# A four-layer attention kernel on one core: x and weight transfers, the q and k projections and the normalisation's small steps placed at other tiles

## The chip, the core and the metric

The kernel runs on one core of a Trainium2 chip. The metric is the device time of one execution in microseconds (us), lower is better; the time before is the median of three runs.

## The reference, cut to what matters

Four layers of multi-head attention with a decomposed relative position bias, each on the group-normalised input and added back to it. Two images of 48x48 tokens, 192 channels, 12 heads of 16 channels.

```python
for layer in range(4):
    h = group_norm(x, groups=32)                 # over a group's 6 channels and all 2304 tokens
    q, k, v = split(h @ Wqkv + bqkv)             # 12 heads of 16
    attn = (q * 16 ** -0.5) @ k.T                # 2304 x 2304 per head and image
    attn += rel_h[:, :, None] + rel_w[:, None]   # q @ Rh, q @ Rw
    x = x + concat(softmax(attn) @ v) @ Wproj + bproj
```

## The kernel before, in words

**Work.** A layer and an image are a stage (8 stages, `s`), a head of a stage is a unit (96 units, `u = 12 s + j`, with `j` the head). A unit is 18 tiles (`t`), each of 128 keys against all 2304 queries. Of each tile TensorE makes five score matmuls (L750; 512, 512, 512, 512, 256 columns), ScalarE takes their exponentials (L535), and one tile later TensorE multiplies them with v (`attend`, L829). In the same tile five more matmuls (L759) form scores of the next unit but one or the next, of which VectorE takes the maxima (L639) that the exponent is shifted by. Scores and maxima alternate through two rings of three PSUM banks, one drained by ScalarE and one by VectorE.

**The written order.** `schedule()` (L53) gives each unit, tile and slot (0 to 5) its items, and TensorE, ScalarE and VectorE all walk the same table. Beside the maxima there are: in tiles 0 to 11 a `rel` item (L775, the bias tables of unit u + 2, copied by ScalarE at L518 and L523); in tile 14 the `mt` item (L781, the maxima turned into a row, written to `mrow` by ScalarE at L545); and `late` items in slot 0 of tiles 12 to 17. These are, by head: 1 and 2, `fin` (output projection of the stage before, L813, added to x by VectorE at L646); 3, `gn` (the normalisation's group sums, L786); 4 to 6, `qk` (projections to q and k of the next stage, L794, copied by ScalarE at L557); 7 and 8, `v` (L802).

**Normalisation.** For the next stage, at head 3, VectorE takes twelve `stat` (L598), one in each of tiles 0 to 11, then `aggregate`, `group_mean`, and at tile 15 `group_scale` (L615), 19 steps on 96x2 elements, each of which waits for the one before (`link`). `normalise` (L630, 96x2304, two of them) runs at head 4, tiles 1 and 2, slot 3, when x has been stored.

**q and k.** ScalarE writes a projection to `stage`, GpSimd splits it into a high and a low part (`split`, L489 and L491), SyncE sends both to `qk_scratch` (`qk_store`, L372). There are two buffers: ScalarE waits for the split two before, the split for the store two before. On GpSimd a unit's six splits come after `normalise(u - 1)` (L481) and the six `low` (L476).

**The transfer queue.** All transfers are issued by SyncE in one written order (L392 to L454). At each tile it waits until the tile's scores are made, then sends a row of bias for three tiles on (`row_load`, L306; needed by the scores of that tile). At tile 3 it loads the first third of the next unit's q and bias (`slot_load`, L312, L314, L306), at tile 15 the second, at 16 the third, and with them the row of maxima (`top_load`, L323, from `mrow`): thirds 0 and 1 at tile 15, 2 at tile 16. Before a unit's tile 0, at head 0, come the load of x (L246, one transfer of 1728 KB) and, every second stage, four transfers of weights (L256); at head 3 the store of x (L252); the last stage's x is loaded ahead of head 8. At tile 12 `image_load`, at 13 and 14 `rel_store`. `qk_store` of heads 4 to 6 stands at tiles 14 to 17 and at tiles 0 and 1 of the next unit.

The excerpt that waits first at a unit's start, from `ready_for_scores` (L730):

```python
if i == 0:
    slot, use = slot_of(u, third)
    pe.wait_ge(slot_in[slot], 144 * use + 64 + 16 * c)   # q, bias, row and mrow of this third
```

Of the kernel before, what the change touches and what calls it, by code (L numbers as in the profile page):

```python
# [40 lines left out]
MSPLIT = SPLIT[-1:] + SPLIT[:-1]  # L41
MT_AT = 2
SLOTS = 4
VCOL = DH + 1
# [8 lines left out]
def schedule():  # L53


    plan = {u: [[[] for _ in range(6)] for _ in range(TILES)] for u in range(-3, UNITS + 2)}

    first = [("gn", 0, 0), ("gn", 0, 1)] + [("qk", 0, m, g) for m in range(3) for g in range(NB)] \
        + [("v", 0, k) for k in range(QT // 2)]
    for k, item in enumerate(first):  # L60
        plan[-3][k // 2][k % 2].append(item)
    for u in range(-2, UNITS):
        for t in range(TILES):
            n, q = (u + 1, t + KEEP) if t < TILES - KEEP else (u + 2, t + KEEP - TILES)
            if 0 <= n < UNITS:
                for m in range(MAXB):
                    plan[u][t][m].append(("max", n, q, m))
            if t < 12 and u + 2 < UNITS:
                plan[u][t][0].append(("rel", u + 2, t))
        if 0 <= u + 1 < UNITS:  # L70
            plan[u][TILES - KEEP][MT_AT].insert(0, ("mt", u + 1))
        s, j = divmod(u, HEADS)
        if u < 0:
            continue
        late = []
        if s >= 1 and j in (1, 2):
            late = [("fin", s - 1, 3 * (j - 1) + g, m) for g in range(3) for m in range(2)]
        elif s + 1 < STAGES and j == 3:
            late = [("gn", s + 1, 0), None, None, ("gn", s + 1, 1)]
        elif s + 1 < STAGES and 4 <= j < 7:  # L80
            late = [("qk", s + 1, j - 4, g) for g in range(NB)]
        elif s + 1 < STAGES and 7 <= j < 9:
            late = [("v", s + 1, k) for k in range(6 * (j - 7), min(6 * (j - 6), QT // 2))]
        for k, item in enumerate(late):
            if item:
                plan[u][12 + k][0].append(item)
    last = [("fin", STAGES - 1, g, m) for g in range(NB) for m in range(2)]
    for k, item in enumerate(last):
        plan[UNITS + 1][k][0].append(item)
    return plan  # L90
# [21 lines left out]
def build(nc, a):  # L112
# [3 lines left out]
    with ExitStack() as ctx:  # L116
# [122 lines left out]
        def _(sp):  # L239
            def x_of(s):  # L240
                l, b = divmod(s, IMAGES)
                src = a["x"] if l == 0 else x_dram
                return src[:, b * N:(b + 1) * N].rearrange("(t p) n -> p t n", t=2)

            def x_load(s):
                sp.dma_start(xb[:, :, :], x_of(s)).then_inc(x_in, 16)  # L246

            def x_store(s):

                sp.wait_ge(dve_read, place["fin", s, NB - 1, 1] + 1)  # L250
                dst = (x_dram if s + IMAGES < STAGES else a["out"])[:, (s % IMAGES) * N:(s % IMAGES + 1) * N]
                sp.dma_start(dst.rearrange("(t p) n -> p t n", t=2), xb[:, :, :]).then_inc(x_stored, 16)  # L252

# [123 lines left out]
            x_load(0)  # L377
            weights(0)
# [13 lines left out]
            for u in range(-2, UNITS):  # L392
                s, j = divmod(u, HEADS) if u >= 0 else (-1, -1)
                if j == 0:
                    sp.wait_ge(for_dve, place["v", s, QT // 2 - 1] + 1)
                    x_load(s - 1 if s else 1)
                    if s % 2 and s + 1 < STAGES:
                        sp.wait_ge(dve_read, place["v", s, QT // 2 - 1] + 1)
                        weights((s + 1) // 2)
                if j == 5 and s % 2 == 0 and s:  # L400
                    sp.wait_ge(for_dve, place["fin", s - 1, NB - 1, 1] + 1)
                    sp.wait_ge(dve_read, place["fin", s - 1, NB - 1, 1] + 1)
                    proj_weights(s // 2)
                if j == 3 and s:
                    x_store(s - 1)
                if u == UNITS - 4:
                    sp.wait_ge(x_stored, 16 * (STAGES - 1))
                    x_load(STAGES - 1)
                for t in range(TILES):
# [15 lines left out]
                    if t == 8 and u >= 0 and u + 2 < UNITS:  # L425
                        mkeys_load(u + 2)
                    if t == 5 and u >= 1:
                        rec_store(u - 1)
# [30 lines left out]
            for g in range(NB):  # L459
                ao_load(STAGES - 1, g)  # L460
            x_store(STAGES - 1)
            sp.wait_ge(x_stored, 16 * STAGES)


        @block.gpsimd
        def _(pool):
# [30 lines left out]
            for u in range(-2, UNITS):  # L497
                s, j = divmod(u, HEADS) if u >= 0 else (-1, -1)
                if u >= 1:
# [72 lines left out]
        def _(dve):  # L572
# [19 lines left out]
            def stat(s, k):  # L592
# [3 lines left out]
                else:  # L596
                    dve.wait_ge(x_in, 16 * (s + 1))
                return dve.bn_stats(stats[:, m, g, :], xb[:, m, g * BLK:(g + 1) * BLK])  # L598
# [15 lines left out]

            def group_scale(bank):  # L615

                link(dve.tensor_scalar(gv[:, :], bank[0:HALF, 0:2], EPS, None, ALU.add))
                link(dve.tensor_scalar(gr[:, :].bitcast(I32), gv[:, :].bitcast(I32), -0.5, SEED, ALU.mult, ALU.add))
                for _ in range(4):
                    link(dve.tensor_tensor(gt[:, :], gr[:, :], gr[:, :], ALU.mult))  # L620
                    link(dve.tensor_tensor(gt[:, :], gt[:, :], gv[:, :], ALU.mult))
                    link(dve.tensor_scalar(gt[:, :], gt[:, :], -0.5, 1.5, ALU.mult, ALU.add))
                    link(dve.tensor_tensor(gr[:, :], gr[:, :], gt[:, :], ALU.mult))
                link(dve.scalar_tensor_tensor(out=gn[:, :], in0=gm[:, :], scalar=-1.0, in1=gr[:, :],
                                              op0=ALU.mult, op1=ALU.mult))

            def normalise(s, m):
                if s >= 2:
                    dve.wait_ge(x_stored, 16 * (s - 1))
                dve.tensor_scalar(xb[:, m, :], xb[:, m, :], gr[:, m:m + 1], gn[:, m:m + 1], ALU.mult, ALU.add)\  # L630
                    .then_inc(xn_ready, 1)

            def consume(item):
# [7 lines left out]
                elif item[0] == "fin":  # L641
                    _, s, g, m = item
                    if g == 0 and m == 0:
                        dve.wait_ge(x_in, 16 * (s + 3 if s + 1 < STAGES else STAGES + 2))
                    xs = xb[:, m, g * BLK:(g + 1) * BLK]
                    dve.scalar_tensor_tensor(out=xs, in0=bank[0:HALF, 0:BLK], scalar=bproj[:, m:m + 1], in1=xs,  # L646
                                             op0=ALU.add, op1=ALU.add).then_inc(dve_read, 1)
                elif item[0] == "gn":
# [3 lines left out]
                    else:  # L652
                        group_scale(bank)
                        dve.sem_inc(dve_read, 1)  # L654
# [37 lines left out]
            for u in range(-3, UNITS + 2):  # L692
                s, j = divmod(u, HEADS) if 0 <= u < UNITS else (-1, -1)
                for t in range(TILES):
                    for i in range(SB + 1):
                        if s + 1 < STAGES and j == 3:
                            if i == 1 and t < 12:
                                last = stat(s + 1, t)
                            if i == 0 and t == 12:
                                aggregate(s + 1, last)  # L700
                        for item in plan[u][t][i]:
                            if item[0] not in ON_ACT:
                                consume(item)
                            if item == ("gn", 0, 1):
                                normalise(0, 0)
                                normalise(0, 1)
# [198 lines left out]
```

## Time and profile before

| what | before |
|---|---|
| median of 3 runs | 7275.24 us (7269.46 to 7281.24) |
| the profiled execution's own time | 7286.74 us |
| its span | 7285.0 us |
| mean granted TensorE clock | 0.978 |
| PE, DVE, ACT, POOL busy | 95%, 75%, 64%, 13% |
| mean DMA rate | 139 GB/s, queue 1 busy 60.8% |

The span runs from the first to the last instruction of one execution; the 1.7 us around it belong to its own time. A busy share is the union of an engine's instructions over the span. TensorE is called PE, VectorE DVE, ScalarE ACT, GpSimd POOL and SyncE's queue SPq. The granted clock is a share of 2.4 GHz.

### The profile page before, as it was taken

The numbers are of one execution on the slowest core, as the hardware profiler recorded it, in microseconds if no ns is written. First come the engines' busy times: TensorE is split into PE (matmuls) and PEld (weight loads), VectorE is DVE, ScalarE is ACT, GpSimd is POOL, SyncE is SP. The second block draws the span as 40 slices with busy tenths as digits, with TensorE's granted clock in tenths as the row PEclk, the third lists the DMA queues.
The fourth block names the chain that finished last, engine by engine and source line by source line (L and its number), as shares of the span: only waits on it lengthen the run. The fifth ranks groups of instructions, "written<-read, shape, count | busy, mean of one in ns | idle before, by whom it ended". The sixth has DMA issues, their size and how long they took to land.

```text
span 7285.0 us, 139171 instructions
## 1 busy us (share of the span) xinstructions
PE 6943.9 (95%) x53600; PEld 4318.7 (59%) x53600; DVE 5490.2 (75%) x10165; ACT 4652.3 (64%) x10033; POOL 931.5 (13%) x967
## 2 busy tenths in 40 slices
PE   6999999999999999999999999999999999999998
PEld 4655656556565565656656566565665656656654
DVE  5776777767777677877878778787777877777773
ACT  2666666666666666666666666666666666666665
POOL 2111111120101101011101111111101021111110
PEclk8999999999999999999999999999999999999999
DMA  5566566556665666656666656666566665566664
GB/s 142 128 138 146 134 139 145 140 141 139 137 152 131 151 130 146 144 133 145 131 147 143 147 137 140 139 152 142 130 141 137 149 145 138 132 146 143 137 135 95
DMA packets 306018, 1013.72 MB, mean 139 GB/s; under 512 B 107152, under 2 KB 196688, under 8 KB 215632
## 3 DMA queue, kind: packets, MB, share of 16 engines
q1 hardware_dynamic: 305360, 1004.81, 60.8%
q8 instruction: 429, 7.03, 0.5%
q14 instruction: 229, 1.88, 0.1%
HBM read 745.26 MB, written 255.69 MB: 137 GB/s over the span
## 4 chain that ended last, share of the span: by engine, by line
PE 88%; DMA 4%; DVE 3%; issue 2%; SPq 2%; POOL 1%; ACT 1%; POOLq 0%; ACTq 0%; DVEq 0%
PE work L759 29%; PE work L750 25%; PE work L829 25%; PE work L775 4%; DMA qk_scratch<-back 2%; DMA moving<-rel_scratch 2%; PE work L813 2%; PE work L794 1%; DVE mpart L639 1%; PE work L802 1%; SPq L372 1%; PE work L781 0%; POOL back L491 0%; ACT back L557 0%; DVE xb L630 0%
## 5 line engine op out<-in xcount | busy, mean ns | idle before, releaser
L639 DVE TENSOR_REDUCE mpart<-work 128x1 f32<-128x512 f32 (+1 forms) x8640 | 5087.1, 632 | 1490.7 <-PE work L759 1472.8
L535 ACT ACTIVATE probs<-work 128x512 f32<-128x512 f32 (+1 forms) x8640 | 4045.6, 558 | 927.5 <-PE work L750 910.4
L750 PE MATMUL work<-moving,keys 113*128 113x512 f32 (+1 forms) x8640 | 3433.3, 398 | 233.7 <-issue 96.1
L759 PE MATMUL work<-mkeys,hi 128*128 128x512 f32 (+1 forms) x8640 | 3472.9, 403 | 32.0 <-DVEq L654 19.3
L759 PEld LDWEIGHTS work<-mkeys,hi 128*128 128x128 f32 x8640 | 1660.5, 192 | 1183.8 <-DVE mpart L639 834.9
L750 PEld LDWEIGHTS work<-moving,keys 113*128 113x128 f32 x8640 | 1657.9, 192 | 778.4 <-ACT probs L535 199.1
L829 PE MATMUL work<-probs,vall 128*17 128x288 f32 x27648 | 2047.7, 415 | 0.0
L829 PEld LDWEIGHTS work<-probs,vall 128*17 128x17 f32 x27648 | 642.0, 97 | 801.7 <-ACT probs L535 226.9
L476 POOL TENSOR_TENSOR full<-full,hi 128x384 f32<-128x384 f32 x576 | 579.7, 1007 | 1662.1 <-DVE hi L682 1662.1
L518 ACT ACTIVATE full<-work 48x384 f32<-48x384 f32 x576 | 279.1, 485 | 642.3 <-PE work L775 642.3
L481 POOL TENSOR_TENSOR rden<-oraw,rden 128x576 f32<-128x576 f32 x96 | 136.2, 1418 | 4167.0 <-DMA rden<-inverse_scratch 4167.0
L523 ACT ACTIVATE full<-work 48x384 f32<-48x384 f32 x576 | 278.9, 484 | 585.2 <-PE work L775 585.2
L775 PE MATMUL work<-image,tab 128*48 128x48 f32 (+1 forms) x6912 | 497.5, 215 | 4.9 <-DMA image<-qk_scratch 4.9
L775 PEld LDWEIGHTS work<-image,tab 128*48 128x48 f32 x6912 | 488.4, 125 | 5.3 <-issue 5.1
L557 ACT ACTIVATE back<-work,bqks,qkscale 128x384 f32<-128x384 f32 x144 | 96.8, 672 | 382.4 <-PE work L794 197.9
L794 PE MATMUL work<-xb,wqk 96*128 96x384 f32 x576 | 217.7, 504 | 11.7 <-DVE xb L630 6.7
L682 DVE CAST hi<-full 128x384 fp32r<-128x384 f32 x576 | 206.7, 359 | 9.1 <-ACT full L523 9.1
L813 PE MATMUL work<-back,wproj 96*96 96x384 f32 x384 | 141.1, 493 | 16.8 <-issue 15.8
L491 POOL TENSOR_TENSOR back<-back,split_hi 128x384 f32<-128x384 f32 x144 | 143.9, 999 | 11.5
L794 PEld LDWEIGHTS work<-xb,wqk 96*128 96x128 f32 x576 | 104.7, 200 | 61.9 <-ACT back L557 10.3
L489 POOL CAST split_hi<-back 128x384 fp32r<-128x384 f32 x144 | 72.6, 504 | 476.9 <-DMA qk_scratch<-back 419.1
L646 DVE SCALAR_TENSOR_TENSOR xb<-work,bproj,xb 96x384 f32<-96x384 f32 x96 | 58.8, 613 | 97.9 <-PE work L813 97.9
(42 smaller groups left out, 633.2 us busy)
## 6 DMA issues: line engine op xcount, KB each, us to landing
moving<-rel_scratch SPq DMA_DIRECT2D x1728, 144.0 KB
moving<-qk_scratch SPq DMA_DIRECT2D x288, 576.0 KB
rel_scratch<-hi SPq DMA_DIRECT2D x192, 432.0 KB, 5.5
rel_scratch<-full SPq DMA_DIRECT2D x192, 432.0 KB, 5.7
moving<-rel_scratch SPq DMA_DIRECT2D x288, 288.0 KB
image<-qk_scratch SPq DMA_DIRECT2D x384, 144.0 KB, 3.2
keys<-qk_scratch SPq DMA_DIRECT2D x192, 288.0 KB, 4.9
qk_scratch<-split_hi SPq DMA_DIRECT2D x144, 192.0 KB, 2.7
```

The lines of the kernel that those rows point to most:

```text
L476: pool.tensor_tensor(full[:, cols], full[:, cols], hi[:, u % 2, cols].bitcast(F32), ALU.subtract)\
L518: act.activation(to, bank[0:SIDE, 0:BLK].rearrange("p (x n) -> p x n", x=NB), ACT.Copy)\
L523: act.activation(to, bank[0:SIDE, 0:BLK].rearrange("p (w h) -> p h w", w=8), ACT.Copy)\
L535: act.activation(probs[:, tile % RING, lo:up], bank[:, 0:up - lo], ACT.Exp).then_inc(act_read, 1)
L639: dve.tensor_reduce(mpart[:, u % 2, q, m:m + 1], bank[:, 0:MSPLIT[m][1] - MSPLIT[m][0]], AX.X, ALU.max)\
L682: dve.tensor_copy(hi[:, u % 2, cols], full[:, cols]).then_inc(hi_ready, 1)
L750: pe.matmul(bank[:, 0:up - lo], tile_of(keys[0:K_ROWS, u % 2, :], c, third), moving[0:K_ROWS, slot_of(u, third)[0], lo:up], start=True, st ...
L759: pe.matmul(bank[:, 0:up - lo], hi[:, u % 2, q * P:(q + 1) * P], mkeys[:, u % 2, lo:up], start=True, stop=True).then_inc(for_dve, 1)
L775: mm = pe.matmul(to, tab[:, layer, d, SIDE - 1 - at:2 * SIDE - 1 - at], query, start=True, stop=True)
L794: mm = pe.matmul(bank[:, 0:BLK], wqk[:, t, m * P:(m + 1) * P], xb[:, t, g * BLK:(g + 1) * BLK], start=(t == 0), stop=(t == 1))
L813: mm = pe.matmul(bank[0:HALF, 0:BLK], wproj[:, t, m * HALF:(m + 1) * HALF], aob[:, k % 2, t, :], start=(t == 0), stop=(t == 1))
L829: mm = pe.matmul(sums[32 * j:32 * j + VCOL, part, 0:QCOL], vall[:, b * QT + t, h, :], probs[:, tile % RING, at:at + QCOL], start=(t == 0), ...
```

## The change

Four things are done, with nothing added to or left out of the computation.

1. **x and weights.** Each transfer of x becomes two, one per half of the channels (`xb[:, m]`). They are issued at tiles 9 and 10 of heads 0 (load), 3 (store) and, in the last stage, 8 (load); the weights at tile 11 of head 0. `top_load` of the next unit's first third goes from tile 15 to tile 14, ahead of the store of `full`.
2. **q and k.** The `qk` items go from slot 0 of tiles 12 to 17 to slot 3 of tiles 1, 3, 5, 7, 9 and 11; `qk_store` to tiles 2, 4, ... 12. On GpSimd three splits come ahead of `normalise(u - 1)`, one behind it, and one each ahead of the second and the fourth `low`.
3. **Normalisation.** Two `stat` in each of tiles 0 to 5 of head 3; the `gn` items in tile 7, slot 4, and tile 9, slot 2; after the latter's first step the other 18 steps one by one, between maxima, from tile 9, slot 3, to tile 12, slot 2.
4. **`normalise`** goes from head 4, tiles 1 and 2, to head 3, tiles 14 and 15, slot 3.

```diff
@@ schedule()
         elif s + 1 < STAGES and j == 3:
-            late = [("gn", s + 1, 0), None, None, ("gn", s + 1, 1)]
+            plan[u][7][4].append(("gn", s + 1, 0))
+            plan[u][9][2].append(("gn", s + 1, 1))
         elif s + 1 < STAGES and 4 <= j < 7:
-            late = [("qk", s + 1, j - 4, g) for g in range(NB)]
+            for g in range(NB):
+                plan[u][QK_AT + 2 * g][3].append(("qk", s + 1, j - 4, g))
@@ block.sync
+            def x_load(s, m):
+                sp.dma_start(xb[:, m, :], src[m * HALF:(m + 1) * HALF, b * N:(b + 1) * N]).then_inc(x_in, 16)
...
-                if j == 0:
-                    sp.wait_ge(for_dve, place["v", s, QT // 2 - 1] + 1)
-                    x_load(s - 1 if s else 1)
-                    if s % 2 and s + 1 < STAGES:
-                        sp.wait_ge(dve_read, place["v", s, QT // 2 - 1] + 1)
-                        weights((s + 1) // 2)
-                if j == 3 and s:
-                    x_store(s - 1)
-                if u == UNITS - 4:
-                    sp.wait_ge(x_stored, 16 * (STAGES - 1))
-                    x_load(STAGES - 1)
...
+                    if j == 0 and t in (9, 10):
+                        sp.wait_ge(for_dve, place["v", s, QT // 2 - 1] + 1)
+                        x_load(s - 1 if s else 1, t - 9)
+                    if j == 0 and t == 11 and s % 2 and s + 1 < STAGES:
+                        sp.wait_ge(dve_read, place["v", s, QT // 2 - 1] + 1)
+                        weights((s + 1) // 2)
+                    if j == 3 and t in (9, 10) and s:
+                        x_store(s - 1, t - 9)
+                    if u == UNITS - 4 and t in (9, 10):
+                        sp.wait_ge(x_stored, 32 * (STAGES - 1))
+                        x_load(STAGES - 1, t - 9)
...
+                    if t == 14 and 0 <= u + 1 < UNITS:
+                        top_load(u + 1, 0)
...
                     if t == 15 and 0 <= u + 1 < UNITS:
                         slot_load(u + 1, 1)
-                        top_load(u + 1, 0)
                         top_load(u + 1, 1)
...
-                    if s + 1 < STAGES and 4 <= j < 7 and t >= 14:
-                        qk_store(s + 1, j - 4, t - 14)
-                    if s + 1 < STAGES and 5 <= j < 8 and t < 2:
-                        qk_store(s + 1, j - 5, t + 4)
+                    if s + 1 < STAGES and 4 <= j < 7 and t > QK_AT and (t - QK_AT) % 2 and t - QK_AT < 2 * NB:
+                        qk_store(s + 1, j - 4, (t - QK_AT) // 2)
@@ block.gpsimd
+                if projecting:
+                    for g in range(3):
+                        split(s + 1, j - 4, g)
                 if u >= 1:
                     normalise(u - 1)
+                if projecting:
+                    split(s + 1, j - 4, 3)
...
                     for r in range(NB):
+                        if projecting and r in (1, 3):
+                            split(s + 1, j - 4, 4 + r // 2)
                         low(u + 2, r)
-                if s + 1 < STAGES and 4 <= j < 7:
-                    for g in range(NB):
-                        split(s + 1, j - 4, g)
@@ block.vector
-                            if i == 1 and t < 12:
-                                last = stat(s + 1, t)
-                            if i == 0 and t == 12:
+                            if i in (1, 3) and t < NB:
+                                last = stat(s + 1, 2 * t + i // 2)
+                            if i == 0 and t == NB:
                                 aggregate(s + 1, last)
...
-                        if s + 1 < STAGES and j == 4 and i == 3 and t in (1, 2):
-                            normalise(s + 1, t - 1)
+                        if s + 1 < STAGES and j == 3:
+                            k = 6 * (t - 9) + i - 3
+                            if 0 <= k < 18:
+                                linked()
+                                group_scale(k)
+                            if i == 3 and t in (14, 15):
+                                linked()
+                                normalise(s + 1, t - 14)
```

`group_scale(k)` is the k-th of the 18 steps, `linked()` the wait for the step before. The counts of `x_in` and `x_stored` double with the number of transfers.

**SyncE around a unit's end, and the load of x.** Before, at the end of a stage (tiles 14 to 17) and the start of the next (tiles 0 and 1):

```order
L328 DMA rel_scratch<-full 48x2304 x2
L312 DMA moving<-qk_scratch 64x1x2304
L314 DMA moving<-rel_scratch 32x2304
L306 DMA moving<-rel_scratch 16x2304
L323 DMA moving<-mrow 1x18x128 x2
L312 DMA moving<-qk_scratch 64x1x2304
L314 DMA moving<-rel_scratch 32x2304
L306 DMA moving<-rel_scratch 16x2304
L323 DMA moving<-mrow 1x18x128
L246 DMA xb<-x_scratch 96x2x2304
L306 DMA moving<-rel_scratch 16x2304 x2
```

Of the change, tiles 9 to 16 of the same head 0:

```order
L248 DMA xb<-x_scratch 96x2304
L354 DMA attention_scratch<-rden 16x576 x4
L308 DMA moving<-rel_scratch 16x2304
L248 DMA xb<-x_scratch 96x2304
L308 DMA moving<-rel_scratch 16x2304 x2
L284 DMA image<-qk_scratch 32x3x384 x4
L308 DMA moving<-rel_scratch 16x2304
L330 DMA rel_scratch<-hi 48x2304 x2
L308 DMA moving<-rel_scratch 16x2304
L325 DMA moving<-mrow 1x18x128
L330 DMA rel_scratch<-full 48x2304 x2
L314 DMA moving<-qk_scratch 64x1x2304
```

x now stands among the rows of tiles 12 to 14, and the first `mrow` has moved ahead of the store of `full` and of the loads of the second third.

**TensorE in a tile with a `qk` item.** Before (tile 14 of a head from 4 to 6), the projection comes right behind `attend` and one maximum:

```order
L829 MATMUL work<-probs,vall 17x288 x8
L759 MATMUL work<-mkeys,hi 128x256
L794 MATMUL work<-xb,wqk 128x384 x2
L750 MATMUL work<-moving,keys 128x512
L759 MATMUL work<-mkeys,hi 128x512
L750 MATMUL work<-moving,keys 128x512
L781 MATMUL work<-ident,mcol 18x128
```

Now (tile 5), behind four maxima and three scores:

```order
L790 MATMUL work<-mkeys,hi 128x512
L781 MATMUL work<-moving,keys 128x512
L790 MATMUL work<-mkeys,hi 128x512
L825 MATMUL work<-xb,wqk 128x384 x2
L781 MATMUL work<-moving,keys 128x512
L790 MATMUL work<-mkeys,hi 128x512
L781 MATMUL work<-moving,keys 128x256
L860 MATMUL work<-probs,vall 17x288 x8
```

**VectorE at head 3.** Before, tile 15, 19 steps in a row (the first seven):

```order
L639 TENSOR_REDUCE mpart<-work 128x1 x6
L617 TENSOR_SCALAR groups<-work 96x2
L618 TENSOR_SCALAR groups<-groups 96x2
L620 TENSOR_TENSOR groups<-groups 96x2
L621 TENSOR_TENSOR groups<-groups 96x2
L622 TENSOR_SCALAR groups<-groups 96x2
L623 TENSOR_TENSOR groups<-groups 96x2
L620 TENSOR_TENSOR groups<-groups 96x2
```

Now, from tile 9 on, one or two between maxima:

```order
L629 TENSOR_SCALAR groups<-groups 96x2
L659 TENSOR_REDUCE mpart<-work 128x1
L634 TENSOR_TENSOR groups<-groups 96x2
L636 TENSOR_TENSOR groups<-groups 96x2
L659 TENSOR_REDUCE mpart<-work 128x1
L638 TENSOR_SCALAR groups<-groups 96x2
L659 TENSOR_REDUCE mpart<-work 128x1
L640 TENSOR_TENSOR groups<-groups 96x2
```

The steps and their order are the same; what stands between them is new.

## Rows read from the trace of the kernel before

**Rows 1.** The page, busy time, and the chain that ended last by line:
```profile
PE 6943.9 (95%) x53600; PEld 4318.7 (59%) x53600; DVE 5490.2 (75%) x10165; ACT 4652.3 (64%) x10033; POOL 931.5 (13%) x967
...
PE work L759 29%; PE work L750 25%; PE work L829 25%; PE work L775 4%; DMA qk_scratch<-back 2%; DMA moving<-rel_scratch 2%; PE work L813 2%; PE work L794 1%; DVE mpart L639 1%; PE work L802 1%; SPq L372 1%; PE work L781 0%; POOL back L491 0%; ACT back L557 0%; DVE xb L630 0%
```
**Rows 2.** Stretches, unit 21 by tile: tiles 10, 12, 16 and 17, and the sum:
```profile
core 0: us, PE busy (x) PEld busy (x) DVE busy (x) ACT busy (x) POOL busy (x), PEclk, DMA share, GB/s
...
1770.95:1774.79 3.84, 3.84 (x39) 2.48 (x37) 3.18 (x7) 2.83 (x6) 1.01 (x1) 1.00 0.29 75
...
1778.28:1781.68 3.40, 3.40 (x28) 2.12 (x27) 3.17 (x7) 2.34 (x5) 1.01 (x1) 1.00 0.15 43
...
1792.40:1795.80 3.40, 3.40 (x28) 2.12 (x27) 2.91 (x5) 2.34 (x5) 0.00 (x0) 1.00 0.95 230
1795.80:1801.83 6.03, 3.75 (x32) 2.38 (x31) 3.33 (x6) 2.83 (x6) 0.00 (x0) 1.00 0.98 187
sum 68.52, PE 66.24 PEld 41.76 DVE 55.04 ACT 47.46 POOL 7.46; mean PE 3.68 PEld 2.32 DVE 3.06 ACT 2.64 POOL 0.41
```
**Rows 3.** Waits of PE: total us, times, longest us:
```profile
PE work L750 <- issue: 96.1, 47, 3.9
PE work L750 <- ACT back L557: 80.5, 35, 4.3
PE work L750 <- DMA moving<-rel_scratch: 52.2, 9, 8.7
...
PE work L759 <- DVEq L654: 19.3, 7, 2.8
```
**Rows 4.** Timeline where unit 21 ends: start us, us, what:
```profile
1794.95 1.61 SPq L323 DMA_DIRECT2D moving<-mrow  x2
...
1801.83 0.47 PE L750 MATMUL work<-moving,keys 113*128 113x512 f32 x1 [2.28 <-issue]
```
**Rows 5.** Stretches, units 22 (tiles 0 and 1) and 23 (tile 0):
```profile
1801.83:1805.49 3.66, 3.66 (x30) 2.37 (x31) 2.48 (x4) 2.34 (x5) 0.00 (x0) 1.00 0.97 160
1805.49:1809.36 3.87, 3.87 (x34) 2.28 (x32) 3.55 (x7) 2.68 (x6) 0.00 (x0) 1.00 0.36 68
...
1870.35:1875.54 5.19, 5.19 (x30) 2.83 (x31) 2.53 (x4) 2.56 (x5) 0.00 (x0) 0.67 0.77 135
```
**Rows 6.** Stretches, unit 36 (stage 3, head 0), tiles 2 and 3:
```profile
2839.37:2851.90 12.53, 3.82 (x35) 2.41 (x32) 3.33 (x6) 3.16 (x7) 0.00 (x0) 0.84 0.98 158
2851.90:2858.44 6.54, 6.54 (x31) 3.85 (x31) 2.77 (x4) 2.78 (x5) 0.00 (x0) 0.51 0.25 59
```
**Rows 7.** DMA issues: KB each, median us to landing:
```profile
xb<-x_scratch SPq DMA_DIRECT2D x6, 1728.0 KB, 16.8
```
**Rows 8.** Stretches, unit 17 (head 5), tiles 12 and 16:
```profile
1472.77:1477.60 4.83, 4.83 (x33) 2.71 (x31) 3.18 (x6) 2.90 (x6) 1.01 (x1) 1.00 0.16 43
...
1492.60:1503.29 10.69, 7.88 (x32) 4.14 (x31) 3.10 (x5) 3.13 (x6) 2.99 (x4) 0.68 0.90 210
```
**Rows 9.** Waits of POOL and of ACT in the q and k chain:
```profile
POOL split_hi L489 <- DMA qk_scratch<-back: 419.1, 67, 11.6
...
ACT back L557 <- POOL back L491: 184.4, 47, 6.4
```
**Rows 10.** Stretches, unit 15 (head 3), tiles 1, 15, 16; unit 16, tile 2:
```profile
1276.29:1280.62 4.33, 3.92 (x34) 2.28 (x32) 4.00 (x8) 2.79 (x6) 0.00 (x0) 1.00 0.71 261
...
1329.79:1337.16 7.37, 4.57 (x29) 2.18 (x28) 5.83 (x24) 2.56 (x5) 0.00 (x0) 0.92 0.64 160
1337.16:1341.55 4.39, 4.39 (x27) 2.84 (x27) 3.05 (x5) 2.56 (x5) 0.00 (x0) 0.75 0.93 204
...
1352.66:1356.78 4.12, 3.91 (x35) 2.22 (x32) 4.12 (x7) 2.81 (x6) 0.00 (x0) 1.00 0.16 42
```
**Rows 11.** Timeline of unit 15, tile 15: two of the 19 steps:
```profile
1332.15 0.16 DVE L620 TENSOR_TENSOR groups<-groups 96x2 f32<-96x2 f32 x1
1332.34 0.16 DVE L621 TENSOR_TENSOR groups<-groups 96x2 f32<-96x2 f32 x1
```

More of the change, by code:

```diff
@@ L42 @@
 MT_AT = 2
+QK_AT = 1
 SLOTS = 4
@@ L239, in _, with x_store @@
         def _(sp):
-            def x_of(s):
+            def x_load(s, m):
                 l, b = divmod(s, IMAGES)
                 src = a["x"] if l == 0 else x_dram
[L243 to L252, printed above, removed]
+                sp.dma_start(xb[:, m, :], src[m * HALF:(m + 1) * HALF, b * N:(b + 1) * N]).then_inc(x_in, 16)
+            def x_store(s, m):
+                sp.wait_ge(dve_read, place["fin", s, NB - 1, m] + 1)
+                dst = (x_dram if s + IMAGES < STAGES else a["out"])[m * HALF:(m + 1) * HALF]
+                sp.dma_start(dst[:, (s % IMAGES) * N:(s % IMAGES + 1) * N], xb[:, m, :]).then_inc(x_stored, 16)
             def weights(l):
@@ L376, in _ @@
                 sp.dma_start(dst, a[name]).then_inc(const_in, 16)
-            x_load(0)
+            x_load(0, 0)
+            x_load(0, 1)
             weights(0)
@@ L460, in _ @@
                 ao_load(STAGES - 1, g)
-            x_store(STAGES - 1)
-            sp.wait_ge(x_stored, 16 * STAGES)
+            x_store(STAGES - 1, 0)
+            x_store(STAGES - 1, 1)
+            sp.wait_ge(x_stored, 32 * STAGES)
         @block.gpsimd
@@ L498, in _ @@
                 s, j = divmod(u, HEADS) if u >= 0 else (-1, -1)
+                projecting = s + 1 < STAGES and 4 <= j < 7
+                if projecting:
+                    for g in range(3):
+                        split(s + 1, j - 4, g)
                 if u >= 1:
                     normalise(u - 1)
+                if projecting:
+                    split(s + 1, j - 4, 3)
                 if u + 2 < UNITS:
                     for r in range(NB):
+                        if projecting and r in (1, 3):
+                            split(s + 1, j - 4, 4 + r // 2)
                         low(u + 2, r)
-                if s + 1 < STAGES and 4 <= j < 7:
-                    for g in range(NB):
-                        split(s + 1, j - 4, g)
+                elif projecting:
+                    split(s + 1, j - 4, 4)
+                    split(s + 1, j - 4, 5)
             normalise(UNITS - 1)
@@ L596, in stat @@
                 else:
-                    dve.wait_ge(x_in, 16 * (s + 1))
+                    dve.wait_ge(x_in, 32 * (s + 1))
                 return dve.bn_stats(stats[:, m, g, :], xb[:, m, g * BLK:(g + 1) * BLK])
@@ L613, in group_mean, with group_scale, linked @@
                 dve.tensor_tensor(gv[:, :], gt[:, :], mv[:, :, 1], ALU.add).then_inc(gn_ready, 1)
[L615 to L625, printed above, removed]
+            def group_scale(k):
+                if k == 0:
+                    step = dve.tensor_scalar(gr[:, :].bitcast(I32), gv[:, :].bitcast(I32), -0.5, SEED, ALU.mult, ALU.add)
+                elif k == 17:
+                    step = dve.scalar_tensor_tensor(out=gn[:, :], in0=gm[:, :], scalar=-1.0, in1=gr[:, :],
+                                                    op0=ALU.mult, op1=ALU.mult)
+                elif k % 4 == 1:
+                    step = dve.tensor_tensor(gt[:, :], gr[:, :], gr[:, :], ALU.mult)
+                elif k % 4 == 2:
+                    step = dve.tensor_tensor(gt[:, :], gt[:, :], gv[:, :], ALU.mult)
+                elif k % 4 == 3:
+                    step = dve.tensor_scalar(gt[:, :], gt[:, :], -0.5, 1.5, ALU.mult, ALU.add)
+                else:
+                    step = dve.tensor_tensor(gr[:, :], gr[:, :], gt[:, :], ALU.mult)
+                links[0] += 1
+                step.then_inc(gn_link, 1)
+            def linked():
+                dve.wait_ge(gn_link, links[0])
             def normalise(s, m):
                 if s >= 2:
-                    dve.wait_ge(x_stored, 16 * (s - 1))
+                    dve.wait_ge(x_stored, 32 * (s - 1))
                 dve.tensor_scalar(xb[:, m, :], xb[:, m, :], gr[:, m:m + 1], gn[:, m:m + 1], ALU.mult, ALU.add)\
@@ L643, in consume @@
                     if g == 0 and m == 0:
-                        dve.wait_ge(x_in, 16 * (s + 3 if s + 1 < STAGES else STAGES + 2))
+                        dve.wait_ge(x_in, 32 * (s + 3 if s + 1 < STAGES else STAGES + 2))
                     xs = xb[:, m, g * BLK:(g + 1) * BLK]
@@ L652, in consume @@
                     else:
-                        group_scale(bank)
+                        links[0] += 1
+                        dve.tensor_scalar(gv[:, :], bank[0:HALF, 0:2], EPS, None, ALU.add).then_inc(gn_link, 1)
+                        linked()
                         dve.sem_inc(dve_read, 1)
@@ L704, in _ @@
                             if item == ("gn", 0, 1):
+                                for k in range(18):
+                                    group_scale(k)
+                                    linked()
                                 normalise(0, 0)
@@ L714, in _ @@
                             top(u + 1)
-                        if s + 1 < STAGES and j == 4 and i == 3 and t in (1, 2):
-                            normalise(s + 1, t - 1)
+                        if s + 1 < STAGES and j == 3:
+                            k = 6 * (t - 9) + i - 3
+                            if 0 <= k < 18:
+                                linked()
+                                group_scale(k)
+                            if i == 3 and t in (14, 15):
+                                linked()
+                                normalise(s + 1, t - 14)
         @block.tensor
```

## The prediction

> **What bounds the kernel now.** I read the page first. TensorE is busy 95% of the span and the chain that ended last runs through its matmuls [rows 1]; the other engines follow it. So only time in which TensorE stands, or runs at the lower clock, can be won. The view of stretches, cut at the first score of each tile, shows its rhythm: in a unit with nothing late a tile of heads 9 to 11 takes 3.84 us with a `rel` item and 3.40 us without, TensorE busy throughout, and the eighteen sum to 68.52 us, 2.4 us of which are the excess of tile 17 (6.03 us against the 3.65 us of a tile that reaches over the `rel` item of the next tile 0) [rows 2]. A unit without a stall is thus 66.1 us. A late projection adds 1.43 us (4.83 against 3.40 us) [rows 2, 8].
>
> The waits of PE name four stalls, all by place [rows 3]: 96.1 us in 47 waits with no releaser named, 80.5 us for ScalarE's copy of a projection, 52.2 us for rows of bias, 19.3 us for VectorE. After a stall the engine runs for some us at the 1.2 GHz level: unit 23's first tile, right behind a boundary stall, was granted 0.67 and took 5.19 us against 3.66 us of unit 22's [rows 5]. I therefore compared the length of each of the 1728 tiles (first score to first score) with its clean length, and price each stall by the sum of excesses, clock included.
>
> **The change part by part.**
>
> Boundary. When unit 21 ends, the two `mrow` transfers are issued at 1794.95 us, behind the second third's loads, and tile 0 of unit 22 starts at 1801.83 us after 2.28 us of standing [rows 4]. Of its four loads only `mrow` is issued this late, so I read "issue" as `mrow`. The excesses of tile 17 and of the next tile 0 sum to 131 us over the stages (idle 96.1 us in 47 boundaries, the rest clock) [rows 3, 5]. One tile earlier, ahead of 864 KB of `rel_store` and the 1008 KB third (1.9 MB, 8 us at 230 GB/s [rows 2]), it lands before it is due: all 131 us go. What is late next is the last third, due at tile 2. In unit 22 the queue is busy 0.97 of tile 0 and 0.36 of tile 1 [rows 5], so its backlog ends near 1806.9 us, and tile 2 starts at 1809.36 us; with 2.28 us less of standing, 0.2 us remain. Some units will therefore stand at tile 2. Bounds: nothing, or all 131 us back. There will be some 70 boundaries without late work (nine heads of twelve, heads 4 to 6 being new among them); I take 0.6 us of standing and 0.3 us of clock in each, nearer to unit 22's margin of about nothing: 63 us.
>
> x. In unit 36 tile 2 takes 12.53 us and tile 3, granted 0.51, 6.54 us, where 3.65 us each are clean [rows 6]: 8.9 and 2.9 us. The row of bias for tile 3 stands in the queue behind 1728 KB of x, which takes 16.8 us to land behind what was already queued [rows 7], and in this stage behind weights too. Over the nine loads (eight stages, and head 8 of the last) the excess is 74 us, of which 52.2 us stand as waits [rows 3]. At tiles 10 to 12 the queue is nearly empty, shares 0.29 and 0.15 [rows 2]: roughly 8.5 us free. x needs 1.77 MB at 230 GB/s [rows 2], 7.7 us, the weights about 2.5 us in three stages. It fits but for some 1.5 us, and each row has two tiles, 7 us, to arrive: all 74 us go. The stores at head 3 are hidden before and after. Bounds: 60 to 74 us won.
>
> Here the row says that queued transfers run on without a pause: tiles 16 and 17 move 230 and 187 GB/s at shares of 0.95 and 0.98 in pieces of 144 to 576 KB [rows 2]. The Trainium skill ("DMA: Bandwidth & Descriptors", Anatomy of one DMA, and Bandwidth) speaks against the split: it gives each DMA about 2.0 us of fixed cost and asks to batch to 1 MiB or more. By that rule the 18 extra transfers would cost 36 us; the sum goes by the row, at nothing.
>
> q and k. Tile 16 of unit 17 takes 10.69 us, granted 0.68, against 4.83 us for a tile with a projection [rows 8]. GpSimd had waited for the store of the split two before, 419.1 us in all, and ScalarE 184.4 us for GpSimd [rows 9]: six projections in six tiles, while the stores stand in the fullest part of the queue and behind `low` on GpSimd. The excesses of tiles 16, 17 and the next 0 in the 21 units sum to 131 us (beyond the projection itself). Now there are two tiles, over 9 us with the projection, per buffer step, and a step is a copy, 1.5 us of GpSimd and a store. The fourth split waits behind `normalise(u - 1)`, but the fifth projection needs the third only. The projections' own 1.43 us stay: 126 of them, same matmuls. In tiles 1 to 11 the 384 KB of a store are 1.9 us of queue at some 200 GB/s. All 131 us go; bounds 65 and 140.
>
> Normalisation. At head 3, tile 15 took 7.37 and tile 16 4.39 us in place of 3.40 [rows 10]: 19 steps, 0.19 us apart [rows 11], with nothing else on VectorE. Seven stages: 35 us, gone. But the steps still take VectorE's time, 5 maxima of a tile being 2.91 us of it [rows 2]. A second `stat` costs 0.46 us, as the first does in tile 1 (4.33 against 3.87 us [rows 5, 10]): tiles 0 and 2 to 5 go to about 3.85 us, 0.2 us each over clean, tile 1 another 0.46. In tiles 9 to 12, 3.18 us with `high` [rows 2] and up to six steps (1.1 us) make 4.3 us: 0.1, 0.5, 0.8 and 0.3 us. `normalise` cost 0.46 us in a tile of 3.65 (4.12 [rows 10]); in tiles of 3.92 and 3.40 us it costs 0.2 and 0.7. Together 4.1 us per stage, less 0.93 us saved at head 4: 3.2, times 7, 22 us. Bounds 12 and 35.
>
> Sum: 131 + 74 + 131 + 35 = 371 us won, 63 + 22 = 85 us paid, net 286 us. The profiled execution took 7286.74 us; 7001 us. It is 11.5 us above the median of the runs shown, which gives 6990 us.
>
> **The rivals.**
>
> (a) The boundary stall stays: the last third is due at tile 2 and the queue, not `mrow`, sets its landing. For it speak the shares of 0.95 to 0.98 at the end of every unit [rows 2, 5]; against it that tile 2 never stood in a unit like 22. All 131 us instead of 63: 7058 us.
>
> (b) q and k still stand, at other tiles: GpSimd comes late to the fourth split because `normalise(u - 1)` waits for its DMA, or ScalarE's extra copy pushes scores. The 131 us stay: 7121 us. Against it, GpSimd was busy 13% [rows 1].
>
> (c) Split transfers have a price, as the page of the skill has it. As a mechanism of this kernel: each of the 18 extra transfers holds the row behind it for 2 us and all of it shows. 7026 us. Tile 16's 230 GB/s [rows 2] speaks against it.
>
> (d) Slower: the stores of q and k now stand in tiles 2 to 12 ahead of rows of bias, and each row that lands late stops TensorE. The tightest row is that of tile 7: between the first third's loads (tile 3) and its need lie three tiles, 11.2 us, and 1008 KB, its own 144 KB and a store's 384 KB make 7.7 us at 200 GB/s. If each of the 126 stores stood for 3.0 us (2 us and the clock), 378 us would be paid: 7368 us. It decides from 286 / 126 = 2.3 us per store on. The 3.5 us of margin speak against it.
>
> That the change does not move what it says can be left aside; the written order shows it.
>
> **How the numbers follow.** Forecast as above 0.70, (a) 0.12, (b) 0.08, (c) 0.05, (d) 0.05. Best bounds together: 371 and 9 more, less 12 and 20 paid, 348 us won, 6927 us. At the other end (a) with the poorer bounds of x, q and k and VectorE, 371 - 131 - 14 - 66 - 35 = 125 us won, 7150 us; cut at 7105 us, since these would have to meet, it leaves (b), (d) and little else out. Range 6930 to 7105 us. Faster by over 0.2% (15 us, about what a measurement of this kernel can tell from no change) takes in the forecast, (a) to (c): 0.94; within 0.2% 0.01; slower 0.05.
>
> **What would show it.** Tile 0 of light units 3.65 us and the first group of PE's waits (47 of "issue") gone or below 20 us; in their place some waits for bias or q at tile 2, of 0.2 to 1.5 us. Head 0: tiles 2 and 3 at 3.65 us, DMA share near 1 in tiles 10 to 12. Heads 4 to 6: 66.1 + 6 x 1.43, near 75 us, POOL's wait for `qk_scratch` near nothing. Head 3 near 70 us, no wait for DVEq. Granted clock above 0.99. Wrong, if the waits named "issue" stay with `mrow` issued early, if waits for rows appear at tiles 7 or 13 to 15, or if tiles 1 to 11 of heads 4 to 6 take more than 5.3 us.

## The result, and the profile after

The changed kernel takes 7101.82 us (median of four runs, 7081.68 to 7122.99), the kernel before 7275.81 us beside it: a ratio of 0.9762, 95% interval 0.9731 to 0.9792. It is faster by 174 us, where 285 us were forecast. The median lies 3 us inside the upper end of the range (7105 us), and two of the four runs lie above it. The profiled execution took 7081.68 us, the shortest of the four, 20 us less than the median.

The page of the changed kernel: busy time, and the chain by line.

```profile
PE 6863.8 (97%) x53600; PEld 4308.7 (61%) x53600; DVE 5489.3 (78%) x10165; ACT 4665.6 (66%) x10033; POOL 934.3 (13%) x967
...
PE work L790 27%; PE work L781 24%; PE work L860 23%; DMA moving<-mrow 10%; PE work L806 4%; PE work L825 2%; PE work L844 2%; PE work L833 1%; DVE mpart L659 1%; SPq L316 1%; SPq L308 0%; PE work L812 0%; SPq L314 0%; DVE xb L650 0%; DMA qk_scratch<-back 0%
```

Its waits of PE (us in total, times, longest us):

```profile
PE work L781 <- DMA moving<-mrow: 127.7, 78, 3.8
...
PE work L790 <- DVE mpart L659: 10.2, 25, 2.1
...
PE work L825 <- ACT back L568: 5.5, 6, 1.0
```

The four stalls of [rows 3], 248 us together, are gone by name. One new wait of 127.7 us stands in their place. Its 78 occurrences lie at the start of 65 of the 96 units: 63 at tile 2, for the last third's loads (113 us), and 15 at tile 1, for the middle third's (15 us). A tenth of the chain is now `DMA moving<-mrow`, where [rows 1] had none. The stretches of the same unit boundary as in [rows 2, 5] (unit 21's tile 17, unit 22's tiles 0, 1 and 2; columns as there) tell where it stands:

```profile
1744.23:1747.82 3.59, 3.59 (x32) 2.31 (x31) 2.91 (x5) 2.34 (x5) 0.00 (x0) 1.00 1.00 207
1747.82:1751.45 3.63, 3.63 (x34) 2.35 (x32) 2.91 (x5) 2.68 (x6) 0.00 (x0) 1.00 1.04 215
1751.45:1757.34 5.89, 4.04 (x35) 2.32 (x32) 3.97 (x8) 3.16 (x7) 0.00 (x0) 1.00 0.65 91
1757.34:1761.02 3.68, 3.68 (x31) 2.40 (x31) 2.48 (x4) 2.34 (x5) 0.00 (x0) 1.00 0.17 44
```

Tile 17 fell from 6.03 to 3.59 us, and tile 1, which ends with the first score of tile 2, rose from 3.87 to 5.89 us. The timeline of that place (start us, us, what) names the row of maxima of the last third, sent at 1746.57 us, as what tile 2 waits for:

```profile
1746.57 0.80 SPq L325 DMA_DIRECT2D moving<-mrow  x1
...
1757.34 0.50 PE L781 MATMUL work<-moving,keys 113*128 113x512 f32 x1 [1.85 <-DMA moving<-mrow]
```

Elsewhere the change did what was forecast. In the next fence are, of stage 3's head 0, tiles 11 and 12 (x and weights in transfer); of unit 17, tiles 3 (with a projection) and 16; of unit 15, tiles 9 and 15.

```profile
2797.41:2800.90 3.49, 3.49 (x31) 2.13 (x29) 3.03 (x6) 2.83 (x6) 1.00 (x1) 1.00 1.05 254
2800.90:2804.29 3.39, 3.39 (x27) 2.11 (x27) 3.16 (x7) 2.34 (x5) 1.01 (x1) 1.00 0.97 206
...
1391.80:1396.72 4.92, 4.92 (x38) 3.11 (x36) 3.00 (x5) 3.36 (x7) 1.15 (x2) 1.00 0.80 168
1446.10:1449.50 3.40, 3.40 (x27) 2.12 (x27) 2.91 (x5) 2.34 (x5) 0.00 (x0) 1.00 0.92 238
...
1269.60:1273.90 4.30, 4.30 (x40) 2.63 (x39) 3.70 (x9) 2.90 (x6) 1.01 (x1) 1.00 0.54 96
1292.40:1296.26 3.86, 3.67 (x27) 1.97 (x27) 3.86 (x7) 2.45 (x5) 0.00 (x0) 1.00 0.84 213
```

x fills tiles 11 and 12 of the queue (1.05 and 0.97, against 0.15 for tile 12 in [rows 2]; a share can pass 1, since it counts a packet's whole time where the packet starts) and no tile is longer for it. The 12.53 us of [rows 6] and the 10.69 us of [rows 8] have no counterpart; tile 15 of head 3 takes 3.86 us, not 7.37 [rows 10].

### The profile page after: what moved, and what is told of

Same layout as the page of the kernel before. It is cut to its first block, busy times and chain, and to the rows that moved or that the text cites. A ratio compares the mean times of both kernels' runs of the same rounds, so it can differ in the third digit from the quotient of the medians.

```text
span 7079.9 us, 139198 instructions
## 1 busy us (share of the span) xinstructions
PE 6863.8 (97%) x53600; PEld 4308.7 (61%) x53600; DVE 5489.3 (78%) x10165; ACT 4665.6 (66%) x10033; POOL 934.3 (13%) x967
## 4 chain that ended last, share of the span: by engine, by line
PE 84%; DMA 11%; DVE 2%; SPq 2%; issue 1%; ACT 0%; POOL 0%; POOLq 0%; DVEq 0%; ACTq 0%
PE work L790 27%; PE work L781 24%; PE work L860 23%; DMA moving<-mrow 10%; PE work L806 4%; PE work L825 2%; PE work L844 2%; PE work L833 1%; DVE mpart L659 1%; SPq L316 1%; SPq L308 0%; PE work L812 0%; SPq L314 0%; DVE xb L650 0%; DMA qk_scratch<-back 0%
## 5 line engine op out<-in xcount | busy, mean ns | idle before, releaser
L781 PE MATMUL work<-moving,keys 113*128 113x512 f32 (+1 forms) x8640 | 3401.8, 395 | 132.7 <-DMA moving<-mrow 127.7
L860 PE MATMUL work<-probs,vall 128*17 128x288 f32 x27648 | 2025.1, 411 | 0.0
L494 POOL TENSOR_TENSOR back<-back,split_hi 128x384 f32<-128x384 f32 x144 | 144.6, 1004 | 11.5
```

The lines of the kernel that those rows point to most:

```text
L781: pe.matmul(bank[:, 0:up - lo], tile_of(keys[0:K_ROWS, u % 2, :], c, third), moving[0:K_ROWS, slot_of(u, third)[0], lo:up], start=True, st ...
L860: mm = pe.matmul(sums[32 * j:32 * j + VCOL, part, 0:QCOL], vall[:, b * QT + t, h, :], probs[:, tile % RING, at:at + QCOL], start=(t == 0), ...
```

## The experiments

Eleven kernels. The first four, the normalisation among them, do one part of the change alone on the kernel before; the others take the new wait apart. Ratios are to the kernel before, with 95% intervals.

**e1_mrow: the boundary's edit alone.**

```diff
+                    if t == 14 and 0 <= u + 1 < UNITS:
+                        top_load(u + 1, 0)
...
                         slot_load(u + 1, 1)
-                        top_load(u + 1, 0)
```

> The kernel before, with one edit: the row of maxima for the next unit's first third is sent at tile 14 instead of 15. Queue theory (the last third of the next unit's loads lands when the backlog of tiles 13 to 17 has drained, whatever TensorE does): the 47 waits of 96 us named 'issue' vanish, waits of 1 to 2 us for the last third appear at tile 2 of the same units, and of the 131 us of the boundary most comes back: 7220 to 7270 us. Margin theory (the prediction's: tile 2 has about as much margin as tile 0 stood): 0.6 us of standing per boundary, 7275 - 131 + 47 x 0.9 = about 7186 us.

Measured: 1.0015 (1.0004 to 1.0027), median 7295 us against 7286 us. The edit that was priced at 131 us won gives nothing; the queue theory had its waits right, but its time (7220 to 7270 us) still too low. Its waits of PE:

```profile
PE work L751 <- ACT back L558: 99.2, 34, 5.4
PE work L751 <- DMA moving<-mrow: 76.6, 46, 3.9
PE work L751 <- DMA moving<-rel_scratch: 67.8, 9, 9.6
```

The 96.1 us of "issue" became 76.6 us for `mrow`, in 46 waits for 47, 44 of them at tile 2. Moving `mrow` alone removed the waits named "issue", so they were waits for it, as the prediction read them. Of what was left, the wait of the projections grew from 80.5 to 99.2 us and that of head 0 from 52.2 to 67.8 us [rows 3]: TensorE comes some 2 us sooner to work that is no sooner done. The margin theory (7186 us) falls.

**e2_x: x and weights alone.** The `x_load`, `weights` and `x_store` of the change; stores stay ahead of head 3.

> The kernel before, with x sent in two halves and its loads at tiles 9 and 10 (weights at 11); the stores stay ahead of head 3's tile 0. All theories: tiles 2 and 3 of head 0 fall to 3.65 us, 60 to 74 us less: 7201 to 7215 us. If split transfers had a fixed price of 2 us each that shows, 7237 us.

Measured: 0.9912 (0.9893 to 0.993), 64 us less. No wait for `rel_scratch` is left. As expected, a little less won than the 74 us of the sum.

**e3_qk: projections, splits and stores alone**, with `normalise` at tiles 16 and 17 of head 3.

> The kernel before, with the projections to q and k, their splits and stores where the change has them, and normalise at head 3, tiles 16 and 17 (it must be done before head 4's tile 1). The stall of tile 16 goes (131 us), heads 4 to 6 become units that end like heads 9 to 11, with 21 more boundary stalls of about 2.8 us (59 us). Margin theory: about 7275 - 131 + 59 = 7203 us. Queue theory: the same place, but the stores in tiles 2 to 12 add to the backlog, so 3 to 5 us per boundary: 7203 to 7250 us.

Measured: 0.9929 (0.9906 to 0.9953), median 7225 us, 52 us less. It lies in the span of both theories and does not tell them apart. Its waits of PE:

```profile
PE work L755 <- issue: 156.6, 68, 4.7
PE work L755 <- DMA moving<-rel_scratch: 44.5, 9, 7.8
```

The wait for ScalarE is gone, and the boundary's wait has grown from 96.1 us in 47 to 156.6 us in 68 places: 2.0 us each before, and 3.1 us for each of the 21 new ones, behind heads 4 to 6 (65 us together).

**e4_norm: the normalisation alone.**

> The kernel before, with the normalisation alone as the change has it (two stat per tile, gn in tiles 7 and 9, single steps, normalise at head 3, tiles 14 and 15). Tiles 15 and 16 of head 3 lose 35 us over the stages, head 3 and 4 pay about 22: 13 us less than before, between 0 and 25 less.

Measured: 0.9971 (0.996 to 0.9982), 21 us less (13 to 29). The four parts alone come to about +11, -64, -52 and -21 us, together -126 us, against -174 us for the whole: the parts are worth more together.

**a2_mrow15: the change without the boundary's edit** (`top_load(u + 1, 0)` back behind `slot_load(u + 1, 1)` at tile 15).

> The changed kernel with the first third's row of maxima back at tile 15. Series theory (two waits stand one behind the other at each boundary, for this row at tile 0 and for the last third at tile 2, and removing one alone lets the other grow by as much): within 30 us of the change's 7102 us. If the move of the row was worth its 131 us in the change: 7200 to 7230 us.

Measured: 0.9812 (0.9796 to 0.9828), median 7151 us. On top of the other parts the edit is worth 50 us by the medians and 36 us by the ratios to the kernel before beside each, with some 25 us of error. That is far from 131 us; whether it is more than the 30 us of the series theory can't be told.

**a1_hi17: the change, with the store of the high part behind the last third.** This is the test of what sets the new wait.

```diff
-                    if t == 13 and u + 2 < UNITS:
-                        sp.wait_ge(hi_ready, NB * (u + 3))
-                        rel_store(u + 2, hi[:, (u + 2) % 2, :].bitcast(F32), 0, rel_hi_stored)
...
                     if t == 16 and 0 <= u + 1 < UNITS:
                         slot_load(u + 1, 2)
                         top_load(u + 1, 2)
+                    if t == 17 and u + 2 < UNITS:
+                        sp.wait_ge(hi_ready, NB * (u + 3))
+                        rel_store(u + 2, hi[:, (u + 2) % 2, :].bitcast(F32), 0, rel_hi_stored)
```

> The changed kernel, with the store of the high part of the bias (864 KB per unit) sent at tile 17, behind the next unit's last third, instead of at tile 13. Queue theory: about 4 us of backlog stand behind the last third instead of ahead of it, the waits for mrow at tile 2 (127.7 us in 78) fall below 20 us and the time to 6940 to 7000 us. If instead the row's own latency or SyncE's issuing sets its landing: no change, 7080 to 7120 us. If the store is then late for the loads at tile 3 or delays the rows of tiles 3 to 5: slower than the change.

Measured: 0.9486 (0.9468 to 0.9504), median 6910 us: 192 us less than the change by the medians (201 us by the ratios), and 376 us less than the kernel before. The wait for `mrow`, and the same boundary's tiles 17, 0, 1 and 2:

```profile
PE work L781 <- DMA moving<-mrow: 7.4, 9, 1.4
```

```profile
1702.08:1705.67 3.59, 3.59 (x32) 2.31 (x31) 2.91 (x5) 2.34 (x5) 0.00 (x0) 1.00 1.03 176
1705.67:1709.32 3.65, 3.65 (x35) 2.37 (x32) 2.91 (x5) 2.67 (x6) 0.00 (x0) 1.00 1.00 210
1709.32:1713.22 3.90, 3.90 (x34) 2.31 (x32) 3.56 (x8) 2.67 (x6) 0.00 (x0) 1.00 0.95 262
1713.22:1716.92 3.70, 3.70 (x33) 2.41 (x31) 2.88 (x5) 2.72 (x6) 0.00 (x0) 1.00 0.53 149
```

The same bytes go through the queue: its share is now 0.95 in tile 1 and 0.53 in tile 2, where it was 0.65 and 0.17. The last third lands in time because 864 KB stand behind it, not ahead. Neither the row's own latency nor SyncE's issuing was what held it: in the 46 boundaries between units where tile 0 had stood in the kernel before, the last `mrow` is sent 1.9 us after tile 17's start in the change and 1.7 us here, and it lands 12.9 and 10.6 us after that start, by the last update of the semaphore that its landing raises (the trace has the time of each). That is 2.3 us sooner, not the 4 us that were expected for 864 KB. The gain in time is above the range expected (6940 to 7000 us), for the clock is better too: 0.995 granted over the span, against 0.988 and 0.978.

**a4_extra: the change, with 432 KB more in the queue at tile 13.** It sends rows of `mkeys` to a spare scratch that nothing reads.

> The changed kernel, with one more transfer of 432 KB per unit (constant rows of mkeys to a spare scratch that nothing reads) at tile 13. Queue theory: 2 us more of backlog at each of some 70 boundaries, each microsecond of it standing, and the clock: the waits for mrow go from 128 to 250 to 290 us, the time to 7240 to 7310 us. If the landing is set by a latency or by SyncE's issuing: within 30 us of the change.

Measured: 0.9955 (0.994 to 0.997), median 7251 us, 149 us more than the change by the medians (141 us by the ratios).

```profile
PE work L788 <- DMA moving<-mrow: 231.5, 116, 4.8
```

The time is in the expected span, the wait a little under it: 104 us more, at the start of 75 units for 65, with the clock at 0.978 for 0.988. In the same 46 boundaries the last third lands 14.6 us after tile 17's start, 1.7 us later than in the change. Less ahead of the last third and more ahead of it both move the time: the queue theory holds.

**a3_hi17_mrow15: a1 without the boundary's edit.**

> The kernel a1_hi17 with the first third's row of maxima back at tile 15. Queue theory: with 4 us less of backlog ahead of it the row lands about 1.7 us after tile 17 has begun, 2 us before it is due, so its place in the order is worth nothing: 6905 to 6925 us. Order theory (the move of this row removes the 131 us of the boundary, which the wait for mrow at tile 0 caused): 7000 to 7040 us.

Measured: 0.963 (0.9614 to 0.9646), median 7015 us. The queue theory, as I had put it here, is wrong: with the store out of the way the first third's row still comes too late at tile 15, and the edit is worth 105 us. By its semaphore the row lands 4.8 us after tile 17's start in those 46 boundaries (5.7 us in the kernel before), where 1.7 us had been expected; it is due 3.6 us after that start.

```profile
PE work L780 <- issue: 82.5, 69, 2.7
```

```profile
1719.98:1724.66 4.68, 3.75 (x32) 2.37 (x31) 3.33 (x6) 2.83 (x6) 0.00 (x0) 1.00 1.02 201
```

69 waits of 1.2 us stand where [rows 3] had 47 of 2.0 us; tile 17 is 4.68 us where [rows 2] had 6.03. Of the old stall of 2.0 us the store ahead made some 0.9 us; the late place in the order is enough for the rest.

**b1_before_hi17 and b2_before_both: the store's move on the kernel before**, alone and with the boundary's edit.

> The kernel before, with only the store of the high part sent at tile 17 instead of 13. Queue theory: the boundary's 131 us go without the change's move of mrow, and the stores of q and k at tiles 14 to 17 land sooner, so a part of their 131 us too; the load of x at head 0 may cost more, since 4 us of stores now stand right ahead of it: 7080 to 7170 us. Order theory: boundary stays, about 7275 us.

> The kernel before with both edits of the boundary: the row of maxima at tile 14 and the store of the high part at tile 17. Alone they gave +0.15% and -0.4%. Series theory: together far more than the sum, the boundary's 131 us and some of the wait for the stores of q and k: 7110 to 7160 us. If the effects add: 7250 to 7265 us.

Measured: b1 0.9957 (0.9942 to 0.9971), 31 us less, and b2 0.9914 (0.9899 to 0.9929), 63 us less. Both expectations fall: both edits do more together than the 20 us of their sum, but only 63 us are left of the 131 us and more. The waits of PE in b2, and head 0 of stage 3, tile 2:

```profile
PE work L751 <- ACT back L558: 102.9, 37, 5.4
PE work L751 <- DMA moving<-rel_scratch: 96.3, 16, 11.4
```

```profile
2817.27:2832.53 15.26, 3.86 (x30) 2.44 (x31) 2.91 (x5) 3.01 (x7) 0.00 (x0) 0.75 0.95 175
```

Of the waits at a boundary, 3.8 us for `mrow` are left, and none named "issue". But the store of the high part and x now follow each other in the queue: tile 2 takes 15.26 us for 12.53 [rows 6], seven places more wait for a row of bias (16 for 9 [rows 3]), and the projections wait 102.9 us for 80.5. Half of what the boundary gives (131 us) the two old stalls take: 44 us more for rows of bias and 22 us more for the projections leave 65 us, and 63 us were measured. That they grow because TensorE reaches them sooner, and the queue is no emptier, is how I read it; no run separates it.

**a5_hi17_whole: a1 with x in one piece, at tile 9.**

> The kernel a1_hi17 with x loaded and stored whole, at tile 9, instead of in halves at tiles 9 and 10 (18 transfers fewer). If a split transfer has no price: 6905 to 6920 us, unless 7.7 us of x in one piece hold the rows of tiles 13 and 14 up. If each extra transfer costs 2 us that show: 36 us less, 6874 us.

Measured: 0.9522 (0.9508 to 0.9536), median 6939 us: 29 us more than in halves. Waits of PE, and head 0 of stage 3, tile 12:

```profile
PE work L785 <- DMA moving<-rel_scratch: 16.4, 9, 3.2
```

```profile
2739.13:2743.47 4.34, 3.55 (x27) 2.08 (x26) 3.62 (x8) 2.34 (x5) 1.01 (x1) 1.00 0.99 179
```

A row of bias is held up behind 1728 KB in each of the nine loads, 1.8 us each and the clock. In halves a row goes between them. An extra transfer has no price that shows here; the split pays.

The eight kernels that vary the two edits, as medians in us:

| | kernel before | with the other parts of the change |
|---|---|---|
| neither | 7286 | 7151 (a2) |
| `mrow` at tile 14 | 7295 (e1) | 7102 (the change) |
| store of the high part at tile 17 | 7253 (b1) | 7015 (a3) |
| both | 7224 (b2) | 6910 (a1) |

By these medians the `mrow` edit gives -9, 29, 50 and 105 us, depending on what else is out of the way. The change's 7102 us was measured beside 7276 us for the kernel before, the others beside 7286 us; the 50 us are 36 us by the ratios.

## Why the prediction was right or wrong

**The side and the mechanisms.** Right: all four stalls named in [rows 3] went, each with the part that was to remove it, and no row of bias came late for the stores in tiles 2 to 12 (rival (d)): the waits of the changed kernel have none for `rel_scratch`.

**x, 74 us.** Right: 64 us alone (51 to 78), with no tile longer at the new place.

**q and k, 131 us.** Right in the stall; not seen was that a projection costs less in slot 3 than in slot 0: 4.92 - 3.65 = 1.27 us for 1.43 us [rows 8]. Over 126 projections that is 20 us more. Rival (b) did not come true: the 80.5 us for ScalarE are gone, and the 5.5 us shown above lie in the projections ahead of the first unit, where the kernel before had 4.9 us.

**Normalisation, 35 - 22 = 13 us.** 21 us (13 to 29): the 13 us lie at the edge of the interval. Some 3 us of the gain the prediction had not counted: seven short waits of TensorE for the group sums at head 3 went as well (30.7 us in 8 waits before, 27.5 us in 1 in e4).

**The boundary: the term that was mis-sized.** "Bounds: nothing, or all 131 us back ... I take 0.6 us of standing and 0.3 us of clock in each, nearer to unit 22's margin of about nothing: 63 us." The tiles 0 to 2 of all units of the changed kernel are together 180 us longer than clean (projections taken off), 128 us of it standing and the rest, by what is left over, the lower clock after it: some 2.0 and 0.8 us in each of 65 units, where 0.6 and 0.3 us in each of 70 were taken. In the profiled execution, for which 7001 us were forecast and which took 7081.68 us, these 117 us over the 63 us are more than the whole shortfall of 81 us; the other terms came out better, the projections alone by 20 us. Four things are wrong in the step.

- The landing of the last third was read from the DMA shares. They put the end of unit 22's backlog near 1806.9 us, but the updates of the semaphore that tile 2 waits for end at 1809.15 us. Tile 2 began at 1809.36 us, so its margin was 0.2 us with TensorE's 2.28 us of standing, and 2.1 us too little without. In the change unit 22 waited 1.85 us.
- The landing was held fixed. Over the 46 boundaries that had stood, the margin at tile 2 was 2.3 us on average, against 2.0 us of standing; had the landing stayed, 21 of them would have waited, 20 us in all. But the last third lands 11.7 us after tile 17's start in the kernel before, 12.8 us in e1 and 12.9 us in the change.
- The new light boundaries are worse than the old. Behind heads 4 to 6 tiles 0 to 2 cost 67 us in 21 units, 3.2 us each, behind the others without late work some 2.0 us each. In e3, where `mrow` had not moved, such a boundary stands 3.1 us, against 1.9 us for the others. The last store of a unit's projections was put at tile 12, next to `image_load`, and may be the reason; no run moved it.
- The upper bound was set at what the old stall had cost. A wait that the queue sets is not bounded by the one that it replaces: 180 us came.

So rival (a), with a chance of 0.12 against 0.70 for the forecast, is what happened, and it was mispriced: 7058 us stood there, 7102 us came. That the time still fell into the range is luck: the range's upper end had been cut from 7150 to 7105 us, and the term that carried the doubt exceeded its own bound. That its mechanism is the queue is shown by a1 and a4; that the row's place in the order is a second, separate condition is shown by a3.

**Rival (c)**, a price for each extra transfer: a5 goes the other way, 29 us for the split, and e2 won 64 us (51 to 78) where 38 us would have been left with that price. The 2.0 us stand in the Trainium skill ("DMA: Bandwidth & Descriptors", Anatomy of one DMA) for a DMA that GpSimd issues; SyncE issues these. The Trainium skill ("DMA: Bandwidth & Descriptors", Bandwidth) asks to batch to 1 MiB or more; in this queue, which other transfers must pass, the measurement decides against the larger piece.

**Left open.** The runs do not say why the last third lands some 1.2 us later after a boundary without a stall than after one with a stall, though it is sent 0.6 us sooner. The kernels in which tile 0 still stands (e3, a2) have the early landing too, 11.5 and 11.8 us after tile 17's start. TensorE, being ahead, has the next rows sent sooner into the same queue; whether that is the reason was not tried.

## What to carry to other kernels

When a wait is to be removed, look for what is due next behind it, and measure its margin from the moment at which it would be due without the wait to the last update of its semaphore; the share of busy DMA put the end of a backlog 2.3 us too early here. Where a full queue sets what is due next, an earlier place for a small transfer can give nothing until bytes go behind the urgent ones: here one store moved by four tiles gave 192 us on top of the change and 31 us without it. Price such edits together, since alone they can show zero.

## What the runs showed of the hardware that was not expected

A transfer in two halves, a tile apart, cost less than one in one piece (6910 and 6939 us), where a transfer of 144 KB could go between them: the 16.4 us of waits for it in nine loads are gone. The same two f32 matmuls of 384 columns took 1.27 us of a tile behind three scores and 1.43 us right behind `attend`, with the clock at 1.00 in both. Behind a full queue a transfer of 9 KB took 11.0 us from its issue to the last update of its semaphore (mean of 46 boundaries of the change), and 8.9 us with 864 KB fewer ahead of it (a1).
